# Seven block products in place of eight for the experts' base projection

## The reference

```python
x = x + xattn(layernorm(x), ctx, conv_w, bn_gamma, bn_beta)     # top-k over 64 of 1,601 channels, gates
x = x + attn(layernorm(x), wq, wk, wv, wo)                      # 32 heads, 8 kv heads, rotary, causal
y = layernorm(x)
gate_logits = einsum('bsd,ed->bse', y, gate_w)                  # 8 experts
weights, selected = top_k(gate_logits, 2); weights = softmax(weights)
result = einsum('bsd,od->bso', y, base_w) + base_b              # the base projection, 2048 x 2048
w_full = sum(one_hot(selected, 8) * weights[..., None], axis=2)
low = einsum('bsd,erd->ebsr', y, lora_A)                        # rank 16 for each expert
x = x + result + 2.0 * einsum('ebsr,eor,bse->bso', low, lora_B, w_full)
```

## Time and profile before

| | us |
|---|---|
| median of 3 runs (2184.95, 2185.38, 2185.44) | 2185.38 |
| span of the profiled execution, first to last instruction | 2183.2 |
| PE busy in the span | 1895.6 (87%) |
| DVE busy | 1302.3 (60%) |
| ACT busy | 1126.1 (52%) |
| POOL busy | 1076.3 (49%) |

### The profile page before, as it was taken

The page is one execution under the profiler, slowest core; times in us unless marked ns, Lnnn a source line. Parts: engine busy times, 40 slices in busy tenths (PEclk is TensorE's granted clock), DMA queues, the critical chain, the costliest instruction groups (busy, mean ns, idle before and its releaser), DMA issues. The chain is left out here.

```text
span 2183.2 us, 37919 instructions
## 1 busy us (share of the span) xinstructions
PE 1895.6 (87%) x14321; PEld 1532.8 (70%) x14321; DVE 1302.3 (60%) x2085; ACT 1126.1 (52%) x2525; POOL 1076.3 (49%) x927
## 2 busy tenths in 40 slices
...
GB/s 388 400 394 394 362 356 354 340 346 351 344 32 78 19 87 188 147 86 84 82 178 141 139 140 101 83 88 86 81 197 144 125 161 187 121 129 132 151 145 108
DMA packets 158390, 407.58 MB, mean 187 GB/s; under 512 B 15616, under 2 KB 44544, under 8 KB 156544
## 3 DMA queue, kind: packets, MB, share of 16 engines
...
...
...
## 5 line engine op out<-in xcount | busy, mean ns | idle before, releaser
L1417 POOL TENSOR_TENSOR t<-t,t 128x512 fp32r<-128x512 f32 (+1 forms) x488 | 656.0, 1357 | 654.1 <-ACT t L1410 582.6
L1974 PE MATMUL ps<-t,t 128*128 128x512 f32 x1856 | 735.0, 396 | 11.1 <-POOL t L1417 5.7
L1976 PE MATMUL ps<-t,t 128*128 128x512 f32 x1856 | 723.9, 390 | 0.0
L1975 PE MATMUL ps<-t,t 128*128 128x512 f32 x1856 | 723.4, 390 | 0.0
L1410 ACT ACTIVATE t<-t 128x512 fp32r<-128x512 f32 (+1 forms) x488 | 293.6, 609 | 693.0 <-PE ps L1976 383.8
L796 PE MATMUL ps<-t,t 128*128 128x128 bf16 (+1 forms) x5889 | 401.1, 221 | 168.0 <-DVE t L479 156.1
L796 PEld LDWEIGHTS ps<-t,t 128*128 128x128 bf16 x5889 | 342.0, 100 | 246.8 <-DVE t L479 218.5
L479 DVE TENSOR_SCALAR t<-t,t 128x1601 bf16<-128x1601 f32 x453 | 465.8, 1054 | 4.9 <-PE ps L796 0.3
L708 ACT ACTIVATE t<-t,t 128x1601 int8<-128x1601 f32 x256 | 419.1, 1637 | 7.9 <-DVE t L638 7.8
L1974 PEld LDWEIGHTS ps<-t,t 128*128 128x128 f32 x1856 | 348.8, 188 | 89.7 <-POOL t L1417 9.5
L1976 PEld LDWEIGHTS ps<-t,t 128*128 128x128 f32 x1856 | 348.7, 188 | 73.9
...
## 6 DMA issues: line engine op xcount, KB each, us to landing
t<-ctxT SPq DMA_DIRECT2D x256, 800.5 KB, 6.8
t<-wqkv SPq DMA_DIRECT2D x192, 256.0 KB, 3.1
t<-wo SPq DMA_DIRECT2D x128, 256.0 KB, 4.5
t<-wb SPq DMA_DIRECT2D x128, 256.0 KB, 3.4
t<-xT SPq DMA_DIRECT2D x48, 256.0 KB, 7.1
t<-x1d SPq DMA_DIRECT2D x32, 256.0 KB, 4.8
x2d<-t SPq DMA_DIRECT2D x32, 256.0 KB, 2.0
...
```

Source lines behind the costliest of these rows:

```text
L1417: e.tensor_tensor(wlo[r][:, 0:nk, :], raw[r][:, 0:nk, :], wh[r][:, 0:nk, :].bitcast(F32), ALU.subtract).then_inc(w_lo, 1)
L1974: e.matmul(bank[:, :], wh[r][:, q, :], xl, start=(kt == 0), stop=False)
L1975: e.matmul(bank[:, :], wlo[r][:, q, :], xh, start=False, stop=False)
L1976: m = e.matmul(bank[:, :], wh[r][:, q, :], xh, start=False, stop=(c == NCH[p] - 1 and q == nk - 1))
```

## The change

The base projection is done as a block product with seven multiplications. Inputs (2,048), outputs (2,048) and the two halves of tokens give 2 x 2 blocks, so that the eight products of 1,024 x 1,024 x 512 become seven, of sums and differences of blocks. The two halves of tokens are no longer done one after the other: the part is now one row of stages over m = 0 to 7, each projection 8 inner tiles (2 chunks), some with the lora_B tile as third chunk. In this text k counts the 152 chunks of the experts' part from 0:

| k | stage | chunks a projection | raw loads a full chunk |
|---|---|---|---|
| 0-3 | la, lb (lora_A, half 0) | 2 | 1 |
| 4-19 | p1 | 2 | 1 |
| 20-43 | p2 | 2 + lora_B | 1 |
| 44-61 | p7, with la of half 1 at 52, 53 | 2 | 2 |
| 62-77 | q6 | 2 | 2 |
| 78-103 | q3, with lb of half 1 at 90, 91 | 2 + lora_B | 1 |
| 104-127 | x (one lora_B chunk), then q5, for each m | 1, 2 | 2 in q5 |
| 128-151 | q4 | 2 + lora_B | 2 |

What is new:

- In p7, q6, q5, q4 a chunk's weights are the sum of two loads. The sum is added in place before the split (`weights_sum`, L1548 of the new file): by POOL for odd chunks, by DVE for even ones. There are six raw buffers. The sums of p7 and q6 are stored by ACT's queue (`kept_sums`) and loaded again as one of the two inputs of q6 and q4.
- The sums and differences of activations are formed over the slots (`PARTS_AT`): n3, n2, s1, q3 by DVE on 128 x 2048, their high parts by ACT, and 24 low parts of 128 x 512 by POOL (n3l, q3l, a2l), the other low parts by DVE.
- The layer norm is now multiplied in before the split (g steps, L1857), for both halves.
- The results are collected in SBUF tiles U, V, `last_rc`: by ACT for p1, by DVE for the others. q5 stores two tiles at a time.

```diff
+    for kind in ("p1", "p2", "p7", "q6", "q3"):
+        for m in range(8):
+            if m == 4 and kind in ("p7", "q3"):
+                out += [("la" if kind == "p7" else "lb", 1, 0, 0)]
+            out += [(kind, 0, m, m)]
+    for m in range(8):
+        out += [("x", 0, m, m), ("q5", 0, m, m)]
+    out += [("q4", 0, m, m) for m in range(8)]
...
+PARTS_AT = {24: ["n3a0"], 25: ["n3b0"], 26: ["n3a1", "n3h0"], 27: ["n3b1"], 28: ["n2a0", "n3h1"], 30: ["n2a1", "n2h0"],
...
+    def raw_free(e, n, j):
...
+        before, jb = RAW_BEFORE[n, j]
+        if jb:
+            summed(e, before)
+        else:
+            e.wait_ge(w_lo, before + 1)
+            if before in KEEP_NO:
+                kept_there(e, before)
...
+        for j, src in enumerate(weights_of(*CHUNKS[n])):
+            slot = RAW_OF[n, j]
+            raw_free(e, n, j)
+            if j == 0 and kept_before(n) is not None:
+                kept_there(e, kept_before(n))
+            e.dma_start(raw[slot][:, 0:chunk_rows(n), :], src).then_inc(d_w[slot], 16)
...
+        weights_landed(e, n, 0)
+        weights_landed(e, n, 1)
+        e.tensor_tensor(a[:, :, :], a[:, :, :], b[:, :, :], ALU.add).then_inc(w_sums[n % 2][0], 1)
...
+        if n in KEEP_NO:
+            p, c = CHUNKS[n]
+            kind, _, m, _ = PROJ[p]
+            e.dma_start(kept_sums[0 if kind == "p7" else 1][m][:, 4 * c:4 * c + 4, :], raw[slot][:, :, :]).then_inc(d_keep[slot][0], 16)
...
+        if s[:3] == "n2a":
+            e.wait_ge(v_part, V_NO[f"n3b{g}"] + 1)
+            e.wait_ge(l_scaled, 8)
+            e.tensor_tensor(AF0[:, far, :], AF1[:, far, :], XF0[:, near, :], ALU.subtract).then_inc(v_part, 1)
...
+        if s[:3] == "n3h":
+            e.wait_ge(v_part, V_NO[f"n3b{g}"] + 1)
+            e.activation(XH_[:, near, :], XF0[:, near, :], ACT.Copy).then_inc(a_part, 1)
...
+        if s[:3] == "n3l":
+            e.wait_ge(a_part, A_NO[f"n3h{t // 4}"] + 1)
+            e.wait_ge(v_part, V_NO[f"n2a{t // 4}"] + 1)
+            e.tensor_tensor(XL_[:, t, :], XF0[:, t, :], XH_[:, t, :].bitcast(F32), ALU.subtract).then_inc(p_part, 1)
...
+            if s == "l2" and i:
+                e.wait_ge(p_part, P_NO["a2l7"] + 1)
...
+            if kind == "q5":
+                e.dma_start(out[:, 1, 8 + i, :], last_rc[i][:, :]).then_inc(d_end[0], 16)
+                e.dma_start(out[:, 0, 8 + i, :], U[i][:, :]).then_inc(d_end[0], 16)
...
             for c in range(NCH[p]):
+                if (CH0[p] + c + 4) % 2 and CH0[p] + c >= N_FFN:
+                    weights_sum(e, CH0[p] + c + 4)
                 weights_gpsimd(e, CH0[p] + c + 3)
+                for job, _, s in after_chunk(p, c):
+                    if job == "parts":
+                        parts_gpsimd(e, s)
```

More of the change, by code:

```diff
@@ new lines, in loads_of, with raw_slots @@
+def loads_of(n):
+    return 2 if kind_of(n) in TWO and chunk_rows(n) == 4 else 1
+def raw_slots():
+    cycle = [(N_FFN + j) % 4 for j in range(4)] + [4, 5]
+    out, k = {}, 0
+    for n in range(len(CHUNKS)):
+        for j in range(loads_of(n)):
+            out[n, j] = n % 4 if n < N_FFN else cycle[k % 6]
+            k += n >= N_FFN
+    return out
+RAW_OF = raw_slots()
+RAW_NO, RAW_BEFORE, SUM_NO, KEEP_NO = {}, {}, {}, {}
+_seen, _in, _kept = {}, [0] * 6, [0] * 6
+for (_n, _j), _s in RAW_OF.items():
+    RAW_NO[_n, _j], RAW_BEFORE[_n, _j] = _in[_s], _seen.get(_s)
+    _in[_s] += 1
+    _seen[_s] = (_n, _j)
+    if _j == 1:
+        SUM_NO[_n] = sum(_k % 2 == _n % 2 for _k in SUM_NO)
+    if _j == 0 and kind_of(_n) in KEPT:
+        KEEP_NO[_n] = _kept[_s]
+        _kept[_s] += 1
@@ new lines @@
+PARTS_AT = {24: ["n3a0"], 25: ["n3b0"], 26: ["n3a1", "n3h0"], 27: ["n3b1"], 28: ["n2a0", "n3h1"], 30: ["n2a1", "n2h0"],
+            31: ["s1a0"], 32: ["n2h1"], 34: ["s1a1"],
+            45: ["q3a0"], 46: ["q3b0"], 47: ["q3h0"], 48: ["q3a1"], 49: ["q3b1"], 50: ["q3h1"], 52: ["n2l0"], 54: ["n2l1"],
+            62: ["a2h0"], 63: ["a2h1"], 78: ["s1h0"], 79: ["s1h1"], 80: ["s1l0"], 82: ["s1l1"]}
+for _t in range(8):
+    PARTS_AT.setdefault(29 + _t, []).append(f"n3l{_t}")
+    PARTS_AT.setdefault(54 + _t, []).append(f"q3l{_t}")
+    PARTS_AT.setdefault(64 + _t, []).append(f"a2l{_t}")
@@ new lines @@
+EXPERTS_AT = {47: ["l0"], 48: ["l1"], 73: ["l2"], 74: ["l3"], 75: ["l4"], 76: ["u"], 78: ["ka"], 79: ["kb"], 81: ["kc"], 82: ["x"],
+              83: ["w"], 84: ["w1"], 85: ["r"], 86: ["r1"]}
+PARTS = [s for k in sorted(PARTS_AT) for s in PARTS_AT[k]]
+BY_POOL = ("n3l", "q3l", "a2l")
+V_NO = {s: k for k, s in enumerate(s for s in PARTS if s[2] != "h" and s[:3] not in BY_POOL)}
+A_NO = {s: k for k, s in enumerate(s for s in PARTS if s[2] == "h")}
+P_NO = {s: k for k, s in enumerate(s for s in PARTS if s[:3] in BY_POOL)}
@@ L242, in build @@
     XH_ = at(96 * KB, [NT, HT], F32R)
-    NR = 14
     RS = (CM * 4 + 31) // 32 * 32
@@ L1204, in build @@
     ROWS_A = [6, 8, 10, 10] + [8] * 4
-    PARTS = [2, 2, 2, 4]
-    N_ADDS = [sum(PARTS[:q]) for q in range(5)]
+    PIECES = [2, 2, 2, 4]
+    N_ADDS = [sum(PIECES[:q]) for q in range(5)]
     def gate_buffer(g):
@@ L1684, in ln_vector @@
                 e.tensor_tensor(by8(sinr[:, :]), by8(Rs[:, :]), sinb, ALU.mult).then_inc(tables, 1)
-        if step == "n" and c > 0:
+        if step == "g" and c < 4:
+            e.wait_ge(l_rstd, i + 1)
+            e.tensor_tensor(four(x, c), four(x, c), bc(Rs[:, :], 4), ALU.mult).then_inc(l_scaled, 1)
+        if (step == "n" or step == "g" and i == 1) and c > 0:
             e.wait_ge(l_hi, 4 * i + c)
```

572 lines of the change are left out of this document (422 added, 150 removed).

## The result

The changed kernel takes **2233.52 us**, median of 4 runs (2230.44 to 2235.44), against 2185.41 for the kernel before on the same chip: ratio 1.0217, 95% interval 1.0203 to 1.0232. It is 2.2% slower where 0.3% faster was forecast, and outside the range of 2156 to 2197.

The account below looks back on a forecast made before the run. The prediction took TensorE's issue of matmuls to bound the experts' part. A span of 2183.2 - 44.2 + 16 + 12 + 10 = 2177.0 us, plus 2.2 to the median of the runs, gave 2179 us, range 2156 to 2197.

Parts of the forecast that it names:

- What the change takes away: Experts' part: 192 fewer matmuls at 0.2264 us, 43.5 us, and one DVE operation less at the end, 0.75: 44.2 us.
- Stage p2, 16 us: In p2, the shared DVE and POOL queue delivers chunk 39's low part at 109.3 against 93.6: stall 16 us, bounds 12 to 20.
- Stages p7 and q6, 12 us: In p7 and q6, the shared queue up to a2l7 outlasts TensorE's work: stall 12 us, bounds 5 to 18.
- the sum of 99.1 us: In p7 and q6, DVE and POOL's queued SBUF work up to a2l7, against TensorE's 85.0 us plus 1.8.
- Stage q4, hidden: In q4, the queue holds 3.0 + 1.27 + 0.69 us for each three chunks: hidden, with 1 us to spare.
- Stage x and q5, 10 us: In x and q5, loads behind stores: two periods take 10.2 + 5.4, 7.8 us each instead of 6.1; 10 us, bounds 0 to 14.
- Stage q3, hidden: In q3, single loads: the queue holds 3.0 + 1.4 against 6.1 us for each three chunks, so no stall.
- The g steps under wo: First half, beside TensorE's work under wo: POOL falls behind 0.8 us for each of eight, has 6 to give; hidden.
- the loop through the stored sums: Slower rival, p7 and q6: raw buffers wait for their sum's store, 17 us more, 2196; chance 0.23.
- The waits overlap: Rival: POOL catches up wherever TensorE stalls; stalls of 20 us, 2161, with none 2141; partly hidden case, chance 0.27.
- the two engines do not exclude each other: Rival: DVE and POOL share SBUF freely, first two stalls go, x/q5's stays: 2151; counted in the partly hidden case, 0.27.
- The clock: Listed among signs of being wrong: the clock falls in TensorE's gaps; no size given.

Follow-up runs that it names:

- one load: Changed kernel with p7, q6, q5 and q4 loading one half of each sum, adding and storing nothing for later; output not the reference's: 2175.36 us.
- all sums by VectorE: Changed kernel with every sum of two loads on VectorE, in the slot of chunk n + 3, none on GpSimd: 2203.76 us.
- low part first: Changed kernel with GpSimd making the low part of chunk n + 3 before the sum of chunk n + 4: 2212.71 us.
- stores late as well: Changed kernel with three edits: sums by VectorE, stores two slots later behind the loads, logits and choice of experts moved later: 2183.84 us.
- stores late: Changed kernel with SP issuing the store of a finished projection two slots later, behind the loads: 2216.05 us.
- small sums: Changed kernel with sums adding 4 of the 128 columns of each tile, loads, waits and order kept; output not the reference's: 2205.94 us.
- spread: Changed kernel with sums by VectorE, stores late, jobs moved, and VectorE's and GpSimd's long work spread over more slots: 2168.17 us, median of 4 runs.

## Why the prediction was wrong

*What the change takes away* was right: 192 matmuls fewer; where nothing waits (q4 in the run with one load, excess 0.1) they run at 0.2264 us.

*Stage p2, 16 us*: 15.8 measured, of which 3.1 belong to p7's first chunk, so 12.8, at the low end of the 12 to 20. VectorE and GpSimd do share SBUF exclusively, and taking away four of the long operations and the 8 low parts n3l took 10 of it away. A path that I had not counted (take-out, store, load) made the first 5 us of it, so that 15.8 beside 16 is in part luck. A stretched operation of the changed kernel, VectorE, answers to the earlier trace rows (2.28 us when it waits for nothing):

```profile
1854.13 3.27 DVE L1906 TENSOR_TENSOR t<-t,t 128x2048 f32<-128x2048 f32 x1
```

*Stages p7 and q6, 12 us*: 26.7 beyond the logits. **The step that failed first** is the sum of 99.1 us: it added up busy times of the queue and had GpSimd work without a break. In fact it stood in front of sums (74.8 us from p7 on), and the order that I had printed, the sum ahead of the low part, was weighed for x and q5 only. The order alone is worth 8 us here, all sums by VectorE 15, and 3.1 more each in front of chunk 44. Part of the lateness is the landing: 3.6 us median for the loads of weights and 3.5 for the stored sums in these stages, where I took 2.1 for the latter. Its DMA issues:

```profile
t<-wb SPq DMA_DIRECT2D x29, 256.0 KB, 3.6
kept<-t ACTq DMA_DIRECT2D x16, 256.0 KB, 3.5
```

*Stage q4, hidden*: 9.9, for the most part the same cause; 4.2 with the low part first, 2.8 with the sums on VectorE, 0.2 with the stores late as well, 0.1 with one load.

*Stage x and q5, 10 us*: 24.9. The mechanism was right (8.0 with the stores late, 18.4 with the low part first), the size was not: 17.9 us for two periods on average (starts of x at 2103.7, 2121.0, 2138.1, 2157.3) against 15.6. The landing was not longer than I took (4.46 us against 4.9). My turn was 10.2 + 5.4. The one shown is 18.5: 7.0 us for the 24 matmuls of the q5 (from 2125.00 on, the first seven at the lower clock) where I had 5.4, and 11.5 for the rest.

*Stage q3, hidden*: 11.4. I only counted the queue of that stage. The choice of experts, cut by VectorE's s1l (2.29 us each), let TensorE stand at w for 5.9 us, and the clock fell. The stalls ahead of it were not the reason: with one load they are gone, and TensorE stands at w for 5.9 us too.

*The g steps under wo, "hidden, else 1 to 2 us"*: 8.7 us more than before. The 6 us of lead did not cover them; with a free slot behind each (and l0 later) the excess is that of before. It could have been read off the plan: eight operations of 2.2 us, 17.6 us of VectorE alone, stood within six slots of 2.71, and GpSimd's low parts beside them.

*The rivals.* The slower one, the loop through the stored sums, named the wrong place: with small sums or with the sums by VectorE the stores stay and p7 and q6 have 8.6 and 11.7 beyond the logits in place of 26.7, so the loop was not what held them first. It came to the fore once that was mended (69.5 us of SP's waits in p7 and q6, spread). "The waits overlap" fell, since the stalls came out longer and not shorter, and "the two engines do not exclude each other" fell.

*The clock* stood only among what would make the forecast wrong. It is the cost that stalls brought with them: p2 to q4 spend, by the clocks of the stretches above, some 47 us at 1.2 GHz (x with q5 alone 21), part of them in the waits themselves. The matmuls issued in them took 20 us more than at full clock, 8.8 in x with q5 and 3.1 in p2. Together the stalls were 95 us and not 38.

Open: what of the 7 us that q6 keeps in the best version is the loop through the stored sums, and why p2 keeps 8. And some 12 of the 95 us are neither a wait of TensorE's nor work at the lower clock.
